# Windowed attention and a routed feed-forward layer: buffers for mixed tiles' weights, constant rows written by engines, and six steps moved

## The reference

```python
# attention, 16 heads of 16, each row sees itself and 64 rows back
q, k, v = split(x @ W_attn + b_attn)
scores  = q @ k.T / sqrt(16); mask = (j <= i) & (j >= i - 64)
x = norm(x + (softmax(where(mask, scores, -inf)) @ v) @ W_proj + b_proj, 1e-5)
# routed feed-forward: 8 experts, each row goes to the one with the largest logit
e = argmax(x @ Wr.T)
y = gelu(x @ W1[e] + b1[e]) @ Wo + bo + x          # 256 -> 1024 -> 256
out = norm(x + norm(y, 1e-12) * gamma + beta, 1e-5)  # norm: layernorm over the 256
```

## Time and profile before

| | |
|---|---|
| median of 3 runs | 550.52 us |
| profiled execution, device time | 547.5 us |
| its span, first to last instruction | 545.5 us |
| mean granted TensorE clock | 0.953 of 2.4 GHz |
| PE busy | 494.5 us (91%) |
| DVE, ACT, POOL busy | 421.4, 353.8, 320.6 us |
| DMA moved | 83.72 MB |

### The profile page before, as it was taken

The page is one execution under the profiler, slowest core; times in us unless marked ns, Lnnn a source line. Parts: engine busy times, 40 slices in busy tenths (PEclk is TensorE's granted clock), DMA queues, the critical chain, the costliest instruction groups (busy, mean ns, idle before and its releaser), DMA issues. The chain is left out here.

```text
span 545.5 us, 24637 instructions
## 1 busy us (share of the span) xinstructions
PE 494.5 (91%) x8593; PEld 435.1 (80%) x8593; DVE 421.4 (77%) x1117; ACT 353.8 (65%) x800; POOL 320.6 (59%) x570
## 2 busy tenths in 40 slices
PE   4579999999999999989897899898999999999890
PEld 3458888888888888878786689897999999999780
DVE  3437888898788885886886647899999999888583
ACT  3437777768686785674756487665667667677560
POOL 7801444445453464443526456788888888888584
PEclk9959999999999997997988999999999999999896
DMA  9697676787786968687567112222343266244510
GB/s 209 166 240 190 169 205 183 225 236 183 205 217 184 248 188 219 178 227 175 145 163 194 37 42 80 61 81 71 93 100 96 81 218 228 81 146 156 179 27 14
DMA packets 97353, 83.72 MB, mean 153 GB/s; under 512 B 37447, under 2 KB 88784, under 8 KB 97235
## 3 DMA queue, kind: packets, MB, share of 16 engines
q1 hardware_dynamic: 93874, 73.70, 49.7%
q0 software_dynamic: 3264, 8.41, 4.5%
q10 hardware_dynamic: 96, 0.04, 0.0%
HBM read 43.63 MB, written 23.62 MB: 123 GB/s over the span
## 5 line engine op out<-in xcount | busy, mean ns | idle before, releaser
L1683 PE MATMUL ps<-wo_hi,ks 128*128 128x256 f16 x576 | 129.5, 274 | 4.3 <-DVE ks L1269 4.0
L1701 PE MATMUL ps<-sT_hi,w_hi 128*128 128x128 f16 x496 | 104.9, 220 | 0.4 <-issue 0.4
L1701 PE MATMUL ps<-sT_lo,w_hi 128*128 128x128 f16 x496 | 105.0, 220 | 0.0
L1701 PE MATMUL ps<-sT_hi,w_lo 128*128 128x128 f16 x496 | 105.0, 220 | 0.0
L1146 DVE TENSOR_REDUCE mx<-ps 128x4 bf16<-128x512 f32 x128 | 82.7, 683 | 8.8 <-PE ps L1469 8.2
L666 POOL CAST att_hi<-att 128x256 f16<-128x256 f32 x32 | 12.7, 396 | 123.9 <-DVE att L974 123.9
L1683 PE MATMUL ps<-wo_lo,ks 128*128 128x256 f16 x288 | 78.8, 274 | 0.0
L816 ACT ACTIVATE probs<-ps 128x512 f32<-128x512 f32 x128 | 69.4, 612 | 6.6 <-PE ps L1495 5.9
L1372 PE MATMUL ps<-v_even,probs 128*64 128x17 f32 x1024 | 71.5, 212 | 1.4 <-issue 1.4
L1372 PE MATMUL ps<-v_odd,probs 128*64 128x17 f32 x1024 | 71.5, 212 | 0.3 <-issue 0.3
L1372 PEld LDWEIGHTS ps<-v_even,probs 128*64 128x64 f32 x1024 | 66.8, 141 | 5.1 <-issue 4.5
(11 more groups left out here) (266 smaller groups left out, 1531.4 us busy)
## 6 DMA issues: line engine op xcount, KB each, us to landing
qk_s<-qk_hi SPq DMA_DIRECT2D x64, 128.0 KB, 3.0
w_in<-in_L_ffn_W_dram SPq DMA_DIRECT2D x32, 256.0 KB, 4.0
v_odd<-slots SPq DMA_DIRECT2D x62, 128.0 KB, 2.1
qs<-qk_s SPq DMA_DIRECT2D x16, 384.0 KB, 4.3
ks<-qk_s SPq DMA_DIRECT2D x16, 384.0 KB, 5.2
ks<-qk_s SPq DMA_DIRECT2D x32, 144.0 KB, 3.9
v_even<-v_odd SPq DMA_DIRECT2D x63, 68.0 KB, 4.2
qk_s<-qk_lo SPq DMA_DIRECT2D x32, 128.0 KB, 3.5
```

The source lines that it names most:

```text
L1683: ins = mm(ps_y[p], h[p][hs][:, ic, :], wo[ws][:, ic, :], start=n == 0, stop=n == 3 * IC - 1)
L1701: up_ins = mm(ps_h[1 - p][:, half, col + m * width:col + (m + 1) * width], weights(ws, owners[m], k, ic), sT[1 - p][ss][:, k, at], start=k ...
```

## The change

Three groups of edits.

1. **Weights of mixed tiles.** `w1_mixed` gets three places of four 4 KB pieces instead of two, with rooms in `probs`, the attention weights and the `qk` buffers. Tiles 28, 30, 32 load at j = 20 to 25, two pieces a step; tile 34 reuses the first place and loads one piece a step, at j = 28 to 31.
2. **Constants of the stacks.** POOL builds the constants for all 128 partitions (`ident_w`, `mask_w`, `key_rows`); DVE writes both whole `qs` stacks at its start; ACT, DVE and POOL write whole `ks` windows, four copies for each half as before. `constant_rows` and its six DMAs are gone. SP's first two stack loads wait for the constant writes.
3. **Moved steps.** The W1 steps of ACT and DVE move one iteration later (n = it), SP's load with them (n = it+2); DVE's last low part is early in iteration 31. From it = 28 on, PE's value product comes after the transposes of the maxima, and `turn_attention` comes after `scores_t(1)`. DVE's early table is cut in three, at it = 26 and 27 behind L1231 and at it = 28 ahead of the copy of attT. `write_table` comes before `taken_early`.

```diff
+        wa_split = sb("wa_split", [P, 2, CC, 3 * C + E], f16)
+        qk_room = [sb(f"qk_{s}", [P, 2, 2, CC, 2 * P], f16) for s in ("hi", "lo")]
...
+        spare += [w1_in[:, :].bitcast(f16), wa_room[:, 0:CC * I // 2].bitcast(f16),
+                  probs[:, 0:2, :, :, :].rearrange("p u i e q -> p (u i e q)").bitcast(f16),
+                  wa_split[:, :, :, :].rearrange("p s k n -> p (s k n)")[:, 0:CC * I]]
+        spare += [qk_room[s][:, :, :, :, :].rearrange("p k w m n -> p (k w m n)") for s in range(2)]
+        COPIES = 3
+        w1_mixed = [[[spare[4 * b + 2 * m + s] for s in range(2)] for m in range(PARTS_M)] for b in range(COPIES)]
...
@@ SP, second stage @@
-                    m = j - (MIXED_AT[n] - (8 if n < 2 else 4))
-                    if 0 <= m < PARTS_M:
-                        if n >= 2:
-                            sp.wait_ge(h_done, 2 * MIXED_AT[n - 2] + 2)
+                    per = 1 if n == COPIES else 2
+                    step = j - MIXED_AT[0] - (0 if n == COPIES else 2 * n - 8)
+                    if 0 <= step < 2 * PARTS_M // per:
+                        if n == COPIES:
+                            sp.wait_ge(h_done, 2 * MIXED_AT[0] + 2)
...
+                        m = step * per // 2
                         no = entries(MIXED_AT[n])[m]
                         owner = sp.value_load(expert[0:1, no:no + 1], min_val=0, max_val=E - 1)
-                        for s in range(2):
-                            sp.dma_start(w1_mixed[n % 2][m][s],
+                        for s in range(2) if per == 2 else (step % 2,):
+                            sp.dma_start(w1_mixed[n % COPIES][m][s],
...
@@ SP, start @@
-            constant_rows(0)
...
+                if g < 2:
+                    sp.wait_ge(query_rows_done, g + 1)
+                    sp.wait_ge(window_done[g], 2)
...
-                for n in (0, 1) if it == -2 else (it + 3,) if a_tile(it + 3) and it > -2 else ():
+                n = it + 2
+                if a_tile(n):
...
-                if it == FIRST + 2:
-                    constant_rows(1)
@@ POOL, start: ident_w first, then mask_w (four selects, one more for the rows above), then @@
+            pool.wait_ge(odd_done, 1)
+            link(nc.gpsimd.tensor_scalar(mask_w[low, :], mask_w[low, :], odd[low, :], 1.0 / ONE, ALU.mult, ALU.mult))
+            for b in range(2):
+                link(nc.gpsimd.tensor_copy(
+                    key_rows[:, b, :, :, :], mask_w.unsqueeze(1).unsqueeze(1).broadcast_to([P, STRIPS, CC, P])))
+                nc.gpsimd.affine_select(out=key_rows[high, b, :, :, :], ...).then_inc(last_done, 1)
+                pool.wait_ge(last_done, b + 1)
...
@@ ACT @@
-                n = it + 1
+                n = it
...
-                if it == FIRST + 1:
-                    act.wait_ge(last_done, 1)
-                    for e, t in ((0, 0), (0, 1), (1, 0), (1, 1)):
-                        last = nc.scalar.activation(window_rows(0, 0, e, t), last_rows[:, 0, :, :, :], ACT.Copy)
-                    last.then_inc(window_done[0], 1)
+                if it in (FIRST, FIRST + 1):
+                    act.wait_ge(last_done, 2)
+                    for t in range(2):
+                        last = nc.scalar.activation(window_rows(0, 1, it - FIRST, t), key_rows[:, 1, :, :, :], ACT.Copy)
+                    if it == FIRST + 1:
+                        last.then_inc(window_done[0], 1)
@@ DVE @@
-            nc.vector.memset(ks[0][0:ALIGNED, 0, :, 0:BLK], 0.0).then_inc(zeros_done, 1)
+            dve.wait_ge(ident_w_done, 1)
+            nc.vector.tensor_reduce(odd[:, :], ident_w[:, 0:BLK], AX.X, ALU.max).then_inc(odd_done, 1)
+            for k in range(2):
+                nc.vector.tensor_copy(qs[k][:, :, :], ident_w.unsqueeze(1).broadcast_to([P, HEADS, 2 * P]))\
+                    .then_inc(query_rows_done, 1)
...
+                if it == LAST:
+                    low_weights(it)
                 for t in turned(it):
...
+                    dve.wait_ge(last_done, 1)
+                    for e, t in ((0, 0), (0, 1), (1, 0), (1, 1)):
+                        last = nc.vector.tensor_copy(window_rows(0, 0, e, t), key_rows[:, 0, :, :, :])
+                    last.then_inc(window_done[0], 1)
...
+                if it == EARLY_OF + 4:
+                    early_table(it)
...
+                if a_tile(it) and it < LAST:
+                    low_weights(it)
...
-                if it == EARLY_OF + 2:
-                    early_runs()
-                    early_entries()
                 if it == EARLY_OF + 4:
+                    write_table(0, 0, EARLY)
                     taken_early()
-                    write_table(0, 0, EARLY)
...
+                if it < EARLY_OF + 4:
+                    early_table(it)
@@ PE @@
-                if a_tile(it + 1):
-                    m = it + 1
+                ending = it >= TILES - LEAD
...
+                if a_tile(it + 1) and not ending:
+                    v_product(it + 1)
...
                 if it == LAST:
                     first_up(first_owner, range(IC // 4, IC // 2))
+                elif ending:
+                    v_product(it + 1)
                 elif a_tile(done):
                     turn_attention(done, ps_attT)
...
-                if it == LAST:
+                if ending:
                     turn_attention(done, ps_attT)
```

More of the change, by code:

```diff
@@ L153, in attention_then_routed_ffn @@
         stage = probs[:, :, :, :, :].rearrange("p u i e q -> p (u i e q)").bitcast(f16)
[L154 to L157 removed]
+        mask_w = stage[:, 0:P]
+        ident_w = stage[:, 2 * P:4 * P]
+        odd = stage[:, P:P + 2].bitcast(f32)
+        key_rows = stage[:, 4 * P:4 * P + 2 * PAIRS * P].rearrange("p (b i c n) -> p b i c n", b=2, i=STRIPS, c=CC)
         rden = sb("rden", [P, HEADS], f32)
@@ L588, in _, with of_copies @@
                                     base=0, pattern=[[-1, P]], channel_multiplier=1).then_inc(ident_done, 1)
+            low, high = slice(0, ALIGNED), slice(ALIGNED, P)
+            def of_copies(rows, n):
+                return ident_w[rows, :].rearrange("p (t k) -> p t k", k=n)
+            link(nc.gpsimd.memset(ident_w, 0.0))
+            link(nc.gpsimd.affine_select(out=of_copies(low, BLK), in_=of_copies(low, BLK), compare_op=ALU.not_equal, fill=ONE,
+                                         base=-1, pattern=[[0, 4], [-2, BLK]], channel_multiplier=1))
+            nc.gpsimd.affine_select(out=of_copies(high, BLK), in_=of_copies(high, BLK), compare_op=ALU.not_equal, fill=ONE,
+                                    base=STACK, pattern=[[0, 4], [-1, BLK]], channel_multiplier=1).then_inc(ident_w_done, 1)
+            pool.wait_ge(ident_w_done, 1)
             nc.gpsimd.memset(bqk[:, :], 0.0).then_inc(bqk_clear, 1)
@@ L591, in _ @@
             link(nc.gpsimd.memset(mask_w, 0.0))
-            for sign, base in ((1, STACK), (-1, BLK - STACK)):
-                link(nc.gpsimd.affine_select(
-                    out=mask_w.rearrange("p (t k) -> p t k", k=P), in_=mask_w.rearrange("p (t k) -> p t k", k=P),
-                    compare_op=ALU.is_ge, fill=MASKED, base=base, pattern=[[0, 2], [sign, P]], channel_multiplier=-sign))
-            link(nc.gpsimd.memset(ident_w, 0.0))
-            link(nc.gpsimd.affine_select(
-                out=ident_w.rearrange("p (t k) -> p t k", k=BLK), in_=ident_w.rearrange("p (t k) -> p t k", k=BLK),
-                compare_op=ALU.not_equal, fill=ONE, base=0, pattern=[[0, 4], [-1, BLK]], channel_multiplier=1))
-            nc.gpsimd.memset(zero[:, :], 0.0).then_inc(masks_done, 1)
-            pool.wait_ge(masks_done, 1)
+            for rows, per, first, last in ((low, 2, 1, P - 1), (high, 1, -STACK, P - BLK // 4)):
+                for sign, base in ((1, first), (-1, last)):
+                    link(nc.gpsimd.affine_select(
+                        out=mask_w[rows, :], in_=mask_w[rows, :], compare_op=ALU.is_ge, fill=MASKED, base=base,
+                        pattern=[[sign * per, P]], channel_multiplier=-sign))
+            link(nc.gpsimd.affine_select(out=mask_w[high, :], in_=mask_w[high, :], compare_op=ALU.is_ge,
+                                         fill=0.0, base=MROWS - ALIGNED - 1, pattern=[[0, P]], channel_multiplier=-1))
+            pool.wait_ge(odd_done, 1)
[3 more added lines that the diff above has]
+                    key_rows[:, b, :, :, :], mask_w.unsqueeze(1).unsqueeze(1).broadcast_to([P, STRIPS, CC, P])))
+                nc.gpsimd.affine_select(
+                    out=key_rows[high, b, :, :, :], in_=key_rows[high, b, :, :, :], compare_op=ALU.not_equal, fill=-ONE,
+                    base=ALIGNED - MROWS - STRIPS * b, pattern=[[-1, STRIPS], [-2 * STRIPS, CC], [0, P]],
+                    channel_multiplier=1).then_inc(last_done, 1)
+                pool.wait_ge(last_done, b + 1)
             link(nc.gpsimd.tensor_copy(ident_b[:, :], ident[:, :]))
```

119 lines of the change are left out of this document (47 added, 72 removed).

## The result

The changed kernel takes 559.39 us, median of 5 runs (554.15 to 559.97); the kernel before, beside it, 549.26 (548.55 to 554.35). The ratio is 1.025, 95% interval 1.019 to 1.031. I had said 547.4 us and a range up to 553.5, so it is wrong in sign. The profiled execution took 559.97 us, its span is 558.2 (before 545.5, 12.7 less), its mean granted clock 0.938 (0.953).

What follows compares the result with a forecast made beforehand. PE was taken as the bound, busy 494.5 of 545.5 us, holes also costing half clock. Terms -5.8 + 0.2 - 2.5 + 2.4 + 2.6 = -3.1 gave a median of 547.4 us, 8-in-10 range 540.5 to 553.5.

Steps and rivals of the forecast that it cites:

- I take 0.8 for each of iterations 28, 29 and 30: 2.4: Value product after the maxima's transposes: first score product 0.7 later, turn_attention's 0.3 after it; plus 2.4 us, ends -1 and 3.3.
- a term for the clock to the start and the table: Gains from less half clock: 2 us within the start's 5.8, and 0.7 for the early table around 272 to 282.
- W1's steps elsewhere keep their distances: Outside the start, W1's load stays two iterations ahead of use; only iteration 31 is charged, plus 0.2 us.
- The start, minus 5.8: Kernel start: PE's 3.84 us hole closes and half clock ends sooner, worth 2; together 5.8 us gained, ends 7.7 and 0.
- up to 1.9 later: Start: half of ACT's four ks copies stand ahead of tile 1's high part of queries and keys, delaying it up to 1.9.
- DVE and POOL shut each other out: Rival, start: DVE's qs copies stop POOL for 3.4 us, gain falls from 5.8 to about 0.4; 552.8 us, chance 0.10.
- The early table, minus 2.5: Iteration 27: table steps move behind L1231, PE's wait of 1.77 us goes, clock adds 0.7; ends 0 and 3.5.
- Mixed weights, plus 2.6: Second stage: SP's extra weight pieces make tile 34's rows 2.6 us later at j = 31; ends minus 2.5 and plus 6.
- The second hole: Second stage: tile 33 waits too, its step j = 30 beginning 3.0 us later, rows at 502.4 for 501.08.
- The rival with 0.33, SP's slack and a free product,: SP has slack and the moved product costs nothing: 539.7 us, or 542 to 545 with part of it; chance 0.33.
- The rival that ended slower: SP's queue decides the end at steps j = 24 to 31, tiles 32 to 35 wait in turn: 556.3 us, chance 0.09.

Runs made afterwards that it cites:

- old order of PE: Changed kernel with the value product and the turning of attention back in their old places from iteration 28 on: 551.78 us, ratio 1.001.
- the start part alone: Kernel before plus stack constants made by engines and W1's steps one iteration later, nothing else: 549.34 us, ratio 1.006.
- W1 alone: Kernel before with W1's loads and splits one iteration later, constant rows still transfers: 552.19 us, ratio 1.009.
- unread work: Changed kernel plus 6 matmuls of 256 columns that nobody reads, in PE's waits of iterations 28 to 30: 554.83 us, ratio 1.004.
- the turning late and ACT's maxima first: Kernel before, iterations 28 to 30: attention turned after two score products, ACT copies values after maxima, product in its old place: 557.79 us, ratio 1.025.
- the rows first: Changed kernel with SP issuing the first two slot tiles' rows before the last W1 load: 555.07 us, ratio 1.006.

## Why the prediction was wrong, point by point

- **The failed step: "I take 0.8 for each of iterations 28, 29 and 30: 2.4", ends -1 and 3.3.** The chain was right up to the first score product: the value copy comes after the transposes, PE waits for ACT. It was measured at 10.3 us in the profiled execution, 1.8 of idle time and 8.5 of slower matmuls. Two things were missing. I let `turn_attention` cost its own 0.3; turning late alone cost 2.1 at full clock in the nearest pair of profiles, as it leaves PE's wait whole and puts DVE's copy behind it into the path. The late product, which I had priced, cost next to nothing by itself (1.002). And I gave a term for the clock to the start and the table but none to waits that I was adding myself, in the stretch with the most waits: 27.2 us at half rate instead of 6.8. Of the 15.8 us between forecast and profile (minus 3.1 and plus 12.7), some 8 are this step, 6 the start, 4 the stretch before iteration 26; the second stage gives 2 back.
- **"W1's steps elsewhere keep their distances", plus 0.2: wrong.** I compared load with use, and did not ask what stands behind the load on SP, as I had done for the second stage. The first slot tile's rows do: 1.59 us in the changed kernel. Taken out, the ratio falls from 1.025 to 1.006, and in the old order of PE from 1.001 to 0.990. The clock follows it too, as the profiles sorted below these points show.
- **The start, minus 5.8: measured minus 1.3 at iteration 1 with the start part alone and 0 in the changed kernel's profile.** W1 alone gives 2.6, not 5.8. The hole closes, and the clock of 38 to 42 us is 1.00 instead of 0.78; but waits of 0.70 and 0.61 for the stack and for x take its place, and PE is at half rate from 30 to 35, so that the time won there is worth half. The constants take back 1.3 of it in this pair of profiles and 2.6 by the medians above (47.5 and 44.9). I had left the first stack at 25.97; with the constants made by engines it came at 27.2 to 28.6 in eleven profiles. I had seen ACT's two copies ahead of the high part, "up to 1.9 later", and did not carry them to the first stack. The rival "DVE and POOL shut each other out" came true in kind, 1.75 us beside the two copies and 2.3 in all for my 3.4. It had stood at 0.10. The Trainium skill, "SBUF — State Buffer", section "SBUF: two separate sides", has the exclusive lock; the two POOL instructions that began beside a copy and ended 0.14 after it agree.
- **The early table, minus 2.5: right.** The difference to before falls from 3.9 to 1.9 between iterations 26 and 27, and alone it gives 0.5% (2.6 us). By the medians of the profiles with and without it the stretch from 26 to 28 is 3.4 shorter (17.7 for 21.1). Whether the steps moved to iteration 28 give some of it back is open: alone it took 26.5 us from 28 to 31 at full clock, the mixed weights alone 25.0.
- **Mixed weights, plus 2.6: too high for the end, about right for tile 34.** From iteration 31 to the last idle row the changed kernel loses 0.7 against before, and tile 34 is turned 1.8 later on that count (13.9 - 12.1), with SP's step j = 31 1.5 later (13.6 - 12.1). More profiles say it better. Counted from iteration 31, tile 34 is turned at 194.2 to 195.0 in ten profiles with two places and at 195.4 to 197.9 in ten with three, medians 2.1 apart; tile 35 is 1.3 apart, and the end 1.2 (232.1 for 231.0). So the part costs some 1.2 us, which its own ratio of 0.997 is too coarse to show. The second hole is there in most, but before tile 32, at most 1.06; tile 33 waits 1.61 in one profile and 0.84 in another.
- **The rival with 0.33, SP's slack and a free product,** was half right: the product late alone is 1.002, and SP had some slack, but the turning moved with the product.
- **The rival that ended slower** named SP's queue in the second stage. The sign was its, the place was not: the queue decided at iteration 30.
- **3.9 us before iteration 26** belong to no step: the profile has a wait of 1.90 for a stack at 155.5 us and half clock behind it, and the length of iterations 1 to 27 goes from 226 to 245 us over the profiles of kernels that differ little there. From 1 to 26 the median is 222 us both with W1's steps moved and without.

The half clock in iterations 28 to 31 sorts by the two faults. In the old order of PE with no unread work there are nine profiles. Where the last W1 load stands ahead of the slot rows it lasts 13.7, 14.9 and 17.1 us and the stretch takes 32 to 33; in the six others it lasts 0 to 6.8 and the stretch takes 25 to 28. With the product and the turning both late it had 25 to 31 us in four profiles, 20.5 with the unread work, and 10.2 with the rows first.

What stays open is the share of each move of the order. With the product alone late there were 6.8 us of half clock, with the turning alone late none, and with the turning late and ACT's maxima first 20.5. One profile of each is too few to give the clock's share of each step.

## What to carry to other kernels

When a step is moved on an in-order engine, price what is left without cover in its old place, what waits behind it in the new one, and on each queue that it passes the next thing in line, not only the step's own distance from its use. A hole in PE is to be charged twice, its length and the half clock that may follow, here above all when several came within a few iterations. When single ratios are too coarse, compare one stretch over the profiles of all kernels that share a step: that placed the table, the constants and the mixed weights.

## What the runs showed of the hardware that I had not expected

The granted clock carries the spread of the times. In 25 runs of the kernel before on one chip, the span goes from 543.3 us at a mean clock of 0.973 to 558.1 at 0.948: 15 us, more than this change is worth. So one profile says where the clock fell, and only many runs say what a change costs.

A POOL instruction that began while DVE copied 4096 columns of float16 ended 0.14 to 0.15 us after the copy, four times in two profiles: a fill of 1.16 us for 0.20, and selects of 1.07, 1.13 and 1.08 for 0.29. A fill that had begun 0.11 before the copy took 0.53, as without one (0.51), and that copy took 1.49 where the other three took 1.22 to 1.31.
